# Recommendation tower on one core: rounds of 512 samples, unrolled, with eight tables looked up by matmul

## The reference

```python
e = stack([tbl_f[ids[:, f]] for f in range(26)], axis=1)     # 2048 x 26 x 128
combined = concatenate([x[:, None, :], e], axis=1)           # 2048 x 27 x 128
inter = einsum('bfd,bgd->bfg', combined, combined)           # all dot products of a sample
z = concatenate([x, inter[:, upper triangle]], axis=1)       # 128 + 351 columns
h = concatenate([z, x], axis=1)                              # 607 columns
h = relu(h @ W_top1 + b_top1)                                # 607 x 512
h = relu(h @ W_top2 + b_top2)                                # 512 x 256
y = h @ W_top3                                               # 256 x 1
```

## Time and profile before

| | before |
|---|---|
| median of the timed runs | 489.13 us |
| profiled execution, first to last instruction | 791.1 us |
| time of the profiled execution outside its span | not known |
| mean granted TensorE clock in it | 0.756 |
| TensorE matmul busy | 487.2 us (62%) |
| VectorE busy | 226.9 us (29%) |
| ScalarE busy | 262.0 us (33%) |
| GpSimd busy | 305.1 us (39%) |
| GpSimd idle until TensorE had transposed a tile of rows | 306.7 us |

### The profile page before, as it was taken

One profiled execution on the slowest core, in us unless ns is written; L12 is line 12 of the kernel. 1 busy time (PEld: TensorE's weight loads), 2 busy tenths in 40 slices (PEclk: granted clock), 3 DMA queues, 4 the chain that ended last, 5 costly groups with the idle time before them and its releaser, 6 DMA issues.

```text
span 791.1 us, 8476 instructions
## 1 busy us (share of the span) xinstructions
PE 487.2 (62%) x3016; PEld 424.6 (54%) x3016; DVE 226.9 (29%) x296; ACT 262.0 (33%) x632; POOL 305.1 (39%) x327
## 2 busy tenths in 40 slices
PE   6407566526748086580956719476393855939977
PEld 4306556426637085470855518464282745827866
DVE  3207251222313142321413213133131332313231
ACT  1115131512416033160522615025150432405762
POOL 6751707370442606336072541705327071350000
PEclk8757767666959679596886959768596866958997
DMA  5620202110110101111010110101101020010000
GB/s 128 198 72 11 54 7 55 28 52 9 34 37 19 53 1 45 27 24 46 0 50 20 35 35 9 52 10 40 30 17 50 3 53 17 27 43 1 1 1 0
DMA packets 20003, 27.57 MB, mean 35 GB/s; under 512 B 10940, under 2 KB 13508, under 8 KB 19985
## 3 DMA queue, kind: packets, MB, share of 16 engines
q0 software_dynamic: 10240, 20.99, 10.3%
q1 hardware_dynamic: 9728, 6.32, 2.9%
q10 hardware_dynamic: 16, 0.01, 0.0%
HBM read 27.29 MB, written 0.01 MB: 35 GB/s over the span
## 4 chain that ended last, share of the span: by engine, by line
PE 42%; another core or an unknown queue 22%; issue 20%; ACT 12%; DVE 3%; DMA 0%; ACTq 0%; SPq 0%; DVEq 0%
PE gram L415 16%; PE ring L453 12%; PE ring L372 11%; ACT xt L585 6%; ACT pairs_or_h L606 4%; DVE onehot L705 2%; PE idb L361 1%; PE ring L442 1%; PE ring L476 1%; ACT xt L574 1%; ACT A L592 1%; DMA pairs_t_or_h<-in_ids 0%; DVE A L786 0%; DVE x_or_h_split L772 0%
## 5 line engine op out<-in xcount | busy, mean ns | idle before, releaser
L321 POOL DMA_INDIRECT rows<-in_tbl,ids_tile x320 | 304.3, 951 | 401.6 <-PE ring L400 306.7
L415 PE MATMUL gram<-xt 128*128 128x104 f32 x1024 | 161.4, 318 | 31.6 <-issue 28.3
L415 PEld LDWEIGHTS gram<-xt 128*128 128x128 f32 x1024 | 153.1, 233 | 38.5 <-issue 33.6
L372 PE MATMUL ring<-onehot,table_hi 125*128 125x256 f32 x368 | 113.1, 334 | 37.6 <-DVE onehot L705 31.3
L705 DVE TENSOR_TENSOR onehot<-idb,vrow 125x2048 fp32r<-125x2048 f32 x48 | 110.0, 2292 | 59.8 <-remote 47.2
L453 PE MATMUL ring<-x_or_h_split,w_hi 128*128 128x256 f32 (+1 forms) x384 | 95.6, 322 | 47.9 <-issue 40.2
L785 DVE COPY A<-gram 32x208 f32<-32x208 f32 x64 | 32.2, 503 | 309.6 <-remote 171.3
L591 ACT COPY A<-gram 32x208 f32<-32x208 f32 x64 | 32.4, 506 | 244.4 <-remote 163.9
L453 PEld LDWEIGHTS ring<-x_or_h_split,w_hi 128*128 128x128 f32 (+1 forms) x384 | 74.1, 219 | 64.0 <-issue 56.8
L372 PEld LDWEIGHTS ring<-onehot,table_hi 125*128 125x128 f32 x368 | 79.9, 217 | 48.0 <-issue 40.2
L372 PE MATMUL ring<-onehot,table_lo 125*128 125x256 f32 x368 | 103.7, 308 | 1.4 <-issue 1.4
(11 more groups left out here) (46 smaller groups left out, 272.9 us busy)
## 6 DMA issues: line engine op xcount, KB each, us to landing
rows<-in_tbl,ids_tile POOLq DMA_INDIRECT x320
xt<-in_tbl SPq DMA_DIRECT2D x6, 500.0 KB
rows<-in_r_dense_features SPq DMA_DIRECT2D x16, 64.0 KB
A<-in_W_top SPq DMA_DIRECT2D x2, 256.0 KB
xt<-in_W_top SPq DMA_DIRECT2D x2, 256.0 KB
pairs_or_h<-in_W_top SPq DMA_DIRECT2D x1, 512.0 KB
ids_tile<-in_ids SPq DMA_DIRECT2D x16, 13.0 KB
pairs_t_or_h<-in_ids SPq DMA_DIRECT2D x1, 208.0 KB
```

Source lines behind the costliest of these rows:

```text
L321: pool.indirect_dma_start(rows[:, t % 2, 1 + r, :], None, aps[f"tbl_{f}"], bass.IndirectOffsetOnAxis(ap=ids_tile[:, t, f:f + 1].bitcast(U3 ...
L372: last = pe.matmul(ps[:, 0:HALF], part[:, m, k, :], onehot[:, buf, k, :], start=(k == 0 and part is table_hi), stop=(k == KT - 1 and part ...
L415: last = pe.matmul(gram[:, s % 2, g // PER_BANK, col:col + QUAD * NA], four, cols, start=True, stop=True)
```

## The change

The changed kernel has no hardware loop: four rounds of 512 samples are written out.

- **Tables.** Eight tables are looked up by matmul and 18 gathered. A lookup covers 512 samples: 16 matmuls of 512 columns (L393 of the changed kernel), one `spread_ids` of 512 columns (L380), and a one-hot in two chunks of four table blocks, each 125 x 4 x 512 values on VectorE (L620). The first chunk of a table may be overwritten when TensorE is through with it, the second when the lookup is done; the ids are spread for the next table after the first pair of the second chunk. All eight lookups of a round stand together at its start, with pieces of the perceptron of the round before between them.
- **Rows.** Gathered rows go to a ring of 37 places. A gather waits until the bank of rows that had its place is transposed; at every sixth gather it also waits until TensorE has filled as many banks as a table of work says (`WORK`, `FIRST`, `PER_GATHER`, `progress_for`). The five banks of a tile's transposes stand one by one between the steps of the products of the tile before.
- **`XT` and `A`.** There is one `XT` of 512 samples, and `A` has two buffers, one for each half, so `unblock` of the first half stands between the products of the second. VectorE copies three of four diagonal blocks of a step, ScalarE one; VectorE also takes every second bank of `unblock` for the first halves.
- **The perceptron.** Layers one and two are plain float32 matmuls (L467, L469, L478), four for each block of outputs instead of twelve, and the split copies are gone.
- **Start.** `table_lo` is made on GpSimd (L320), one after every two of the first 16 gathers. Each table comes in two transfers, of 112 and 13 partitions. The ids come transposed from the host (`ids_t`), and the rows of `W_top1` in an order that makes the gathered features neighbours (`w1_order`).

The core of the diff:

```diff
-LOOKUP_TABLES = [2, 5, 10, 12, 13, 14]
+LOOKUP_TABLES = [2, 5, 10, 12, 13, 14, 15, 19]
+ROWS = 37
+GROUP = 6
+FIRST = -41.0
+PER_GATHER = 1.34
...
+    def stages():
+        def rows(r, t, *groups):
+            for g in groups:
+                yield "rows", r, t, g
+        def layer(stage, r, h, *blocks):
+            for n in blocks:
+                yield stage, r, h, n
+        for r in range(NB):
+            first, last = r == 0, r == NB - 1
+            q = r - 1
+            for m in range(NL):
+                yield "lookup", r, m, 0
+                if not first:
+                    if m in (0, 1):
+                        yield from layer("layer2", q, 0, m)
+                    if m == 2:
+                        yield from layer("layer3", q, 0, 0)
+                    if m in (2, 3):
+                        yield from layer("unblock", q, 1, 2 * m - 4, 2 * m - 3)
+                    if m == 4:
+                        yield from layer("pairs", q, 1, 0, 1, 2)
+                    if m in (5, 6):
+                        yield from layer("layer1", q, 1, m - 5)
+                if m in (5, 6):
+                    yield from rows(r, 0, m - 5)
+            yield from rows(r, 0, 2)
+            if not first:
+                yield from layer("layer1", q, 1, 2)
+            yield from rows(r, 0, 3, 4)
+            if not first:
+                yield from layer("layer1", q, 1, 3)
+            yield from rows(r, 1, 0)
+            for s in range(TSTEPS):
+                yield "products", r, 0, s
+                yield from rows(r, 1, s + 1)
+            if not first:
+                yield from layer("layer2", q, 1, 0)
+            for s in range(TSTEPS):
+                yield "products", r, 1, s
+                yield from rows(r, 2, s)
+            yield from rows(r, 2, 4)
+            if not first:
+                yield from layer("layer2", q, 1, 1)
+            for s in range(TSTEPS):
+                yield "products", r, 2, s
+                yield from rows(r, 3, s)
+                yield from layer("unblock", r, 0, s)
+            yield from rows(r, 3, 4)
+            if not first:
+                yield from layer("layer3", q, 1, 0)
+            for s in range(TSTEPS):
+                yield "products", r, 3, s
+                if s == 0:
+                    yield from layer("pairs", r, 0, 0, 1, 2)
+                else:
+                    yield from layer("layer1", r, 0, s - 1)
+            yield from layer("layer1", r, 0, 3)
+            if last:
+                yield from layer("unblock", r, 1, 0)
+                yield from layer("layer2", r, 0, 0)
+                yield from layer("unblock", r, 1, 1, 2)
+                yield from layer("layer2", r, 0, 1)
+                yield from layer("unblock", r, 1, 3)
+                yield from layer("layer3", r, 0, 0)
+                yield from layer("pairs", r, 1, 0, 1, 2)
+                yield from layer("layer1", r, 1, 0, 1, 2, 3)
+                yield from layer("layer2", r, 1, 0, 1)
+                yield from layer("layer3", r, 1, 0)
     RING_STAGES = ("rows", "lookup", "unblock", "pairs", "layer1", "layer2", "layer3")
...
+    WORK = {"rows": 0.44, "lookup": 4.1, "unblock": 0.4, "pairs": 0.25, "layer1": 1.75, "layer2": 1.75, "layer3": 0.9,
+            "products": 1.8}
+    USE = {}
+    DONE = []
+    done = 12.0
+    for stage in stages():
+        done += WORK[stage[0]]
+        if stage[0] in RING_STAGES:
+            USE[stage] = len(USE)
+            DONE.append(done)
...
+    def filled_by(work):
+        return sum(d <= work for d in DONE)
+    def on_vector(r, h, b):
+        return b % 2 == 1 and (h == 0 or r == NB - 1)
...
+            def lower_part(m):
+                pool.wait_ge(hi_ready, m + 1)
+                pool.tensor_tensor(table_lo[:, m], raw[m], table_hi[:, m].bitcast(F32), ALU.subtract).then_inc(lo_ready, 1)
+            def gathers(k):
+                for g, f in enumerate(GATHER_TABLES):
+                    i = k * NG + g
+                    if i >= ROWS and (g == 0 or group_of(i - ROWS) != group_of(i - ROWS - 1)):
+                        pool.wait_ge(ring_filled, filled("rows", *group_of(i - ROWS)))
+                    if i % GROUP == 0 and progress_for(i, k) > 0:
+                        pool.wait_ge(ring_filled, progress_for(i, k))
                     pool.indirect_dma_start(
-                        rows[:, t % 2, 1 + r, :], None, aps[f"tbl_{f}"],
-                        bass.IndirectOffsetOnAxis(ap=ids_tile[:, t, f:f + 1].bitcast(U32), axis=0),
-                    ).then_inc(rows_landed[t % 2], 16)
-            def gathers_after(r, t):
-                pool.wait_ge(filled_rows, USES_X * (4 * r + t + 1))
-                gathers(r, t)
+                        rows[:, i % ROWS, :], None, aps[f"tbl_{f}"],
+                        bass.IndirectOffsetOnAxis(ap=ids_all[:, k, f:f + 1].bitcast(U32), axis=0),
+                    ).then_inc(rows_landed[k % 3][g // GROUP], 16)
+                    if i % 2 == 1 and i // 2 < NL:
+                        lower_part(i // 2)
+            def progress_for(i, k):
+                if k == 0:
+                    return 0
+                return min(filled_by(FIRST + PER_GATHER * i), USE["rows", (k - 1) // T, (k - 1) % T, 0])
+            def group_of(i):
+                k, g = divmod(i, NG)
+                return k // T, k % T, (1 + g) // 4
...
-            def lookup(start, buf, m, ready, col):
-                ps = claim(start)
-                pe.wait_ge(onehot_ready, ready)
-                for k in range(KT):
-                    for part in (table_hi, table_lo):
-                        last = pe.matmul(ps[:, 0:HALF], part[:, m, k, :], onehot[:, buf, k, :],
-                                         start=(k == 0 and part is table_hi), stop=(k == KT - 1 and part is table_lo))
-                    if k == 0 and m + 1 < NL:
-                        spread_ids(m + 1, col)
-                last.then_inc(looked_up, 1)
+            def lookup(r, m):
+                ps = claim("lookup", r, m, 0)
+                u = r * NL + m
+                if r == 0:
+                    pe.wait_ge(lo_ready, m + 1)
+                for c in range(CH):
+                    pe.wait_ge(onehot_ready, CH * u + c + 1)
+                    for k in range(KC):
+                        for part in (table_hi, table_lo):
+                            last = pe.matmul(ps, part[:, m, c * KC + k, :], onehot[:, c, k, :],
+                                             start=(c == 0 and k == 0 and part is table_hi),
+                                             stop=(c == CH - 1 and k == KC - 1 and part is table_lo))
+                        if c == CH - 1 and k == 0 and m + 1 < NL:
+                            spread_ids(r, m + 1)
+                    last.then_inc(first_chunk_used if c == 0 else ring_filled, 1)
...
-            def split_products(ps, blocks, w, x, ready):
-                terms = [(k, rows, wp, xp) for k, rows in blocks for wp, xp in ((0, 0), (1, 0), (0, 1))]
-                for i, (k, rows, wp, xp) in enumerate(terms):
-                    if ready is not None and i % 3 == 0:
-                        pe.wait_ge(*ready[k])
-                    last = pe.matmul(ps, w[wp][0:rows, k], x[xp][0:rows, k, :], start=(i == 0), stop=(i == len(terms) - 1))
-                last.then_inc(filled_mlp, 1)
+            def layer1(r, h, n):
                 if n == 0:
+                    if r + h == 0:
+                        pe.wait_ge(w1_ready, 1)
+                        pe.wait_ge(weights_landed, 16 * N_WEIGHTS)
+                    wait_emptied("pairs", r, h, len(K_PAIR) - 1)
+                ps = claim("layer1", r, h, n)[:, 0:HALF]
+                pe.matmul(ps, w1[:, 0, n * P:(n + 1) * P], x_dense[:, h, :], start=True, stop=False)
+                for k, (k0, w) in enumerate(K_PAIR):
+                    last = pe.matmul(ps, w1[0:w, 1 + k, n * P:(n + 1) * P], x[0:w, k, :], start=False, stop=(k == KX - 1))
...
-            def one_hot(buf, ready, free):
-                dve.wait_ge(idb_ready, ready)
-                if free is not None:
-                    dve.wait_ge(looked_up, free)
-                dve.tensor_tensor(onehot[:, buf], idb[0:VP, 0:HALF].unsqueeze(1).to_broadcast([VP, KT, HALF]),
-                                  vrow[:].unsqueeze(2).to_broadcast([VP, KT, HALF]), ALU.is_equal).then_inc(onehot_ready, 1)
+            def one_hot(r, m, chunks=range(CH)):
+                u = r * NL + m
+                dve.wait_ge(idb_ready, u + 1)
+                for c in chunks:
+                    if u:
+                        if c == 0:
+                            dve.wait_ge(first_chunk_used, u)
+                        else:
+                            dve.wait_ge(ring_filled, filled("lookup", (u - 1) // NL, (u - 1) % NL, 0))
+                    dve.tensor_tensor(onehot[:, c], idb[0:VP].unsqueeze(1).to_broadcast([VP, KC, RS]),
```

(2 more changed lines are left out.)

806 lines of the change are left out of this document (310 added, 496 removed).

## The result

| | before | after |
|---|---|---|
| median of the timed runs | 493.24 us (486.33 to 502.81, 4 runs) | 469.65 us (468.88 to 470.90, 4 runs) |
| ratio | | 0.961, 95% interval 0.955 to 0.967 |
| profiled execution: time, span | 791.1 us span (above) | 469.21 us, 467.4 us |
| mean granted TensorE clock | 0.756 | 0.963 |

The forecast was 465 us. The time outside the span is 1.8 us. The 493.24 us are the three runs ahead of the prediction and one more, of 497.35 us.

The account below looks back on a forecast made before the run. The kernel was taken as a chain on TensorE with ScalarE's and VectorE's hand-overs in it; first round 133 + three rounds of 103 + tail 23 = 465 us, forecast range 450 to 480, chance 0.46.

Parts of the forecast that it names:

- GpSimd's timetable: First round: gather 17 goes at 45 us, the 72nd is issued at 115 and lands at 118; round ends at 133.
- A lower part: Making one table's `table_lo` on GpSimd in the first round was priced at 2.3 us, against VectorE's 1.22.
- VectorE paces the lookups: Lookups: making one-hots takes 5.75 us a table where TensorE has 3.94 us of work.
- A later round: Each of three rounds after the first costs 103 us, with 100.7 us of TensorE's work.
- A 512-column matmul: Lookups on TensorE: 0.215 us each, so 16 matmuls are 3.44 us.
- The last tile's gathers: Later rounds: gathers land at 85 us where TensorE wants them at 86; just in time, costing nothing.
- the tail: The end stage after the last round, with layer two of the first half in it: 23 us.
- rival 3: Same time: lookups at 0.24 a matmul, slower hand-overs, clock falling in first-round gaps; 490 us, range 479 to 492, chance 0.15.
- Rival 1: Gathers are quicker outside the profiler: 451 us at 1.0 us pitch, 439 if never late; range 438 to 451, chance 0.25.
- Rival 2: Slower: gathers become the chain from a pitch of 1.26 us, 500 us at 1.5; range 490 to 510, chance 0.14.
- The fourth: The gathers' new wait for TensorE's progress does nothing and is priced at nothing; part of the forecast, no separate chance.
- The disturbance by bursts: Other engines nearly stand still during gather bursts in the profile; expected again in the new profile, absent from timed runs.

Follow-up runs that it names:

- lower_vector: Changed kernel with the eight lower parts (`table_lo`) made on VectorE instead of GpSimd: 453.75 us, ratio 0.930 to the kernel before; a repeat took 454.43 us.
- before_again: The kernel before, unedited, profiled once more in the undisturbed condition: 489.64 us.
- pitch_150: Changed kernel with a small GpSimd clearing behind each of the 288 gathers; pitch came out at 1.32 us: 486.71 us, ratio 0.991 to the kernel before.
- after_again: The changed kernel itself, unedited, run again and this time in the starved condition: 613.80 us, ratio 0.776 to the kernel before.
- lower_vector_no_hold: Changed kernel with the lower parts on VectorE and without the gathers' wait for TensorE's progress, in the starved condition: 667.53 us, ratio 0.837 to the kernel before.

## Why the prediction was right

**Steps that held.** The first round ends where GpSimd's timetable puts it: gather 17 goes out at 44.58 (forecast 45), behind the eighth lower part, and from there the pitch of 1.25 us carries the gathers to the 72nd; the round ends at 134.3 (133). That undoing the move to GpSimd gives 16 us shows that this timetable set the time, as forecast: in lower_vector the first round ends at 119.3. A lower part costs 2.35 to 2.42 us (2.3), beside VectorE's 1.22: the two are a factor of two apart. The Trainium skill ("GPSIMD Engine Reference", section 8, "Key points") says that VectorE is about twice as fast for such work, and the trace agrees. VectorE paces the lookups of the first round at 5.73 us a table (5.75). A later round takes 103.1 us (103) with 100.3 of TensorE's work (100.7), and TensorE waits for no one-hot in it. The hold caused none of the long waits in the profiled one of the timed runs.

**Errors that cancelled.** Gather 17 was forecast from ScalarE's eighth upper part (43 us, measured 42.0). But GpSimd waited only 0.30 us for that: its own queue, 4.8 us for every two gathers and a lower part, is just as long. The forecast does not add up that queue, and that it comes to the same time is luck. The forecast also counted 56 steps from the 17th gather to the 72nd, where there are 55: that one goes out at 113.7 (115), and the bank of the last gathers follows at 116.3 (118). The four steps behind it took the 15 us forecast; but 2.5 us before them, the rest of the tile's banks and a wait of 1.11 us for ScalarE, had no price. The first table landed near 7 us and, after 4.9 us of TensorE's waiting for its lower part, lookups began at 10.7, not 14; the matmuls of its first chunk stood 0.43 us apart, nearly twice the later 0.23, and the lookups ended at 56.6 (58). A 512-column matmul takes 0.226 us, not 0.215: 1.4 us a round more; yet the sum of TensorE's work came out, 100.7 against 100.3 busy, so other terms were too high by as much; which ones was not followed. The last tile's gathers are not in time but 1.45 us late. The sum missed 1.3 us in the first round, 0.3 in the rounds, 0.8 in the tail and the 1.8 outside the span, 4.2 of the 4.65 us between 465 and 469.65; the profiled execution is 0.4 under the median.

**What I had not priced.** In the first round the clock falls, as rival 3 said of its gaps; against lower_vector it goes with 8.8 us more busy time there, and the forecast still came out since GpSimd's timetable was the longer of the two. Had gathers never been late, the first round would hardly have ended at 107: lower_vector, with 4.7 us of waits left, needed 119.3.

**The rivals.** Rival 1 (gathers quicker outside the profiler) is wrong: before_again has the same pitch in a profiled execution that takes 489.64 us. Rival 2 was the nearest danger: 0.07 us more of pitch cost 15 us, as pitch_150 shows. Rival 3's 0.24 a matmul was wrong (0.226 to 0.230), its clock right; the 21 and the 4 of its sum are not explained there, though its terms, 5.2 in each of three rounds and 10 once, also give 490. The fourth, that the hold does nothing, was true of the runs that were timed and false where gathers starve the rest.

**A reading that failed.** "The disturbance by bursts will be there again" in the new profile: it was not. I took it for something the profiler does in every execution; it is a condition in which all runs of a group stand, timed ones too, and in which the change is worth 22% instead of 4%. The hold is 42 of the 176 us by which the changed kernel is ahead there; the rest I did not take apart.

**How the undisturbed gain divides.** Between the two undisturbed traces, 487.6 and 467.4 us, 0.8 us are gained until the last layer of the first half (151.33 against 150.54), 8.9 over the next two rounds (366.38 against 356.71), 10.5 from there to the last such stage (484.46 against 464.25). The first round gains nearly nothing, and its late gathers are why: in lower_vector the same stage stands at 135.50, 15.8 us before the kernel before. Which of the other edits saves those was not run apart.

## What the runs showed of the chip

The starved condition, in the trace of after_again. GpSimd issues gathers at 1.25 us from 45.1 us on without a pause, and TensorE comes to this:

```profile
78.51 1.98 PE L432 MATMUL gram<-xt 128*128 128x104 f32 x10
81.69 0.25 PE L432 MATMUL gram<-xt 128*128 128x104 f32 x1 [1.20 <-issue]
85.19 0.33 PE L432 MATMUL gram<-xt 128*128 128x104 f32 x1 [3.25 <-issue]
88.00 0.33 PE L432 MATMUL gram<-xt 128*128 128x104 f32 x1 [2.48 <-issue]
90.09 0.33 PE L432 MATMUL gram<-xt 128*128 128x104 f32 x1 [1.76 <-issue]
92.89 0.33 PE L432 MATMUL gram<-xt 128*128 128x104 f32 x1 [2.47 <-issue]
95.69 0.33 PE L432 MATMUL gram<-xt 128*128 128x104 f32 x1 [2.47 <-issue]
...
105.89 3.71 PE L432 MATMUL gram<-xt 128*128 128x104 f32 x16 [2.73 <-DVE A L637]
```

These are single matmuls of one step whose operands had been there since 78.51: the profile names no semaphore between them, yet they come 2.1 to 3.5 us apart, where 16 undisturbed ones take 1.9. The last gather before GpSimd's pause goes out at 96.66; at 104.15 ScalarE and VectorE start at once after 19.87 and 48.12 us of waiting. GpSimd itself is not slowed, 946 ns a gather in both conditions, and in the slices from 61 to 92 us the DMA engines move 51 and 56 GB/s, as in the undisturbed trace. So the profile shows neither a semaphore nor a landing, and the gathers' own rate is unchanged. That the supply of instructions is held up behind the gathers would fit, and was not tested. The Trainium skill ("Runtime: NRT & Kernel Launch", section "The ~15µs preamble/postamble breakdown") says that instructions are prefetched through a port of their own; no run here shows whether that path is the one held up.

It takes unbroken gathers. In after_again the lookups of the first round, with lower parts between the gathers, are spared: the last pair of matmuls starts at 56.5 us, undisturbed at 56.0. In lower_vector_no_hold, where the gathers follow each other from the start, the same pair starts at 87.3 us, after waits of 6.64, 7.41 and 13.51 us. Unrolled and looped kernels both suffer from it. What puts a group of runs in this condition is open: two groups had the same chip number and opposite conditions.

In these traces a wait of TensorE costs more than its length: 7.8 us of landing waits fewer went with 8.8 us less busy time (clock 0.82 to 0.94), and 2.3 more in a round with 1.6 more (1.00 to 0.98).

## What to carry to other kernels

When one engine's queue sets when the first data of a pipeline is complete, anything placed in that queue can cost twice: its own time, and, where TensorE is the engine that waits, what the clock takes from it, here 7.8 and 8.8 us. Look for an engine with idle time in just that stretch; here VectorE had it, and 453.75 us against 469.65 was the price of eight short instructions. And when a profile and the timed runs disagree by half, run the unchanged kernel again before believing either: here both were true, of two conditions, and a wait that is worth nothing in one is worth 42 us in the other.
